# bf16 class value products, earlier loads for both attentions, and idle products around the stage boundaries

## The reference, cut to what matters

```python
h = _L0_tok_ref(x, weight, weighted_sum)                 # (8, 512, 256)
h = concatenate([broadcast(cls_tok), h], axis=1)         # (8, 513, 256)
h = h + _L0_attn_ref(_layernorm(h), ...)    # layernorm, masked product, 16 heads of 16, relu attention, MLP
h = h + _L0_ffn_ref(_layernorm(h), ...)     # fp4-quantized gated MLP, 704 wide
h = h + _L1_attn_ref(_layernorm(h), ...)    # conv, scan over the sequence, gate
h = h + _L1_ffn_ref(_layernorm(h), ...)     # softmax attention + top-2 of 8 experts

# causal attention of layer 0
att = relu(q @ k.T / 4) * tril(ones); att = att / (sum(att) + 1e-9); ctx = att @ v
# attention of the last layer
attn = softmax(q @ k.T / 4); attn_out = attn @ v
```

## Time and profile before

| | |
|---|---|
| median of 3 runs | 2316.9 us (2316.5 to 2319.5) |
| the profiled execution | 2317.53 us, span of the trace 2315.7 us |
| mean granted PE clock | 0.955 of full speed |
| PE / DVE / ACT / POOL busy | 92% / 69% / 39% / 29% |
| qkv | about 172 to 312 us |
| causal | 315 to 556 us |
| mlp, fp4 | 557 to 870, 871 to 1194 us |
| ssm_in and scan | 1195 to 1383 us |
| moe | 1384 to 1800 us |
| attend | 1801 to 2316 us |

### The profile page before, as it was taken

The page is one execution under the profiler, slowest core; times in us unless marked ns, Lnnn a source line. Parts: engine busy times, 40 slices in busy tenths (PEclk is TensorE's granted clock), DMA queues, the critical chain, the costliest instruction groups (busy, mean ns, idle before and its releaser), DMA issues. The chain is left out here.

```text
span 2315.7 us, 40942 instructions
## 1 busy us (share of the span) xinstructions
PE 2132.0 (92%) x11635; PEld 1349.1 (58%) x11635; DVE 1591.6 (69%) x4349; ACT 898.2 (39%) x2108; POOL 677.5 (29%) x1282
## 2 busy tenths in 40 slices
PE   7998969998999997999978949999999899999998
PEld 6877833334888885666653327888888223333332
DVE  3336846664777766888858856777776778888881
ACT  1114635553122224444424422222222067777777
POOL 3554525553333422333321101111111311111111
PEclk9998979998999999999989969999999589999999
DMA  3324664552000000000010001112212512222210
GB/s 126 117 86 94 150 183 131 139 138 89 1 0 0 0 0 14 0 0 0 0 54 9 9 27 38 43 40 46 46 38 45 141 34 75 75 75 75 75 43 20
DMA packets 215001, 131.95 MB, mean 57 GB/s; under 512 B 117186, under 2 KB 203916, under 8 KB 214924
## 3 DMA queue, kind: packets, MB, share of 16 engines
q1 hardware_dynamic: 214924, 131.01, 21.1%
HBM read 89.51 MB, written 40.93 MB: 56 GB/s over the span
## 5 line engine op out<-in xcount | busy, mean ns | idle before, releaser
L2474 DVE TENSOR_REDUCE attend_mx<-ps 128x1 f32<-128x512 f32 x512 | 326.0, 683 | 71.7 <-PE ps L2195 70.3
L2332 ACT ACTIVATE keep_x<-ps 128x512 f32<-128x512 f32 x512 | 280.7, 596 | 125.4 <-PE ps L2209 123.9
L1839 PE MATMUL ps<-keep_early,moe_zT 128*128 128x256 f32 x1056 | 243.3, 384 | 6.4 <-DVE keep_h L1994 4.4
L1839 PEld LDWEIGHTS ps<-keep_early,moe_zT 128*128 128x128 f32 x1056 | 196.5, 191 | 43.1 <-DVE keep_h L1994 18.6
L2195 PE MATMUL ps<-attend_ks,keep_o 96*128 96x512 bf16 x512 | 209.4, 414 | 9.0 <-DVE attend_mx L2474 4.7
L2209 PE MATMUL ps<-keep_o,attend_ks 99*128 99x512 bf16 x512 | 191.9, 384 | 2.2 <-ACT keep_x L2332 2.2
L857 DVE SCALAR_TENSOR_TENSOR keep_early<-ps,causal_causal 128x512 f32<-128x512 f32 (+3 forms) x256 | 114.1, 486 | 82.9 <-PE ps L737 82.8
L1994 DVE SCALAR_TENSOR_TENSOR keep_h<-ps,moe_g,keep_h 128x256 f32 (+1 forms) x264 | 127.5, 483 | 61.1 <-PE ps L1839 52.7
L2195 PEld LDWEIGHTS ps<-attend_ks,keep_o 96*128 96x128 bf16 x512 | 50.4, 99 | 195.9 <-DVE attend_mx L2474 148.9
L827 POOL TENSOR_TENSOR keep_early<-keep_early,causal_causal 128x128 f32<-128x128 f32 x256 | 113.0, 457 | 131.8 <-ACT keep_early L796 130.8
L796 ACT ACTIVATE keep_early<-ps 128x512 f32<-128x512 f32 (+3 forms) x256 | 98.5, 435 | 129.1 <-PE ps L737 128.9
(11 more groups left out here) (325 smaller groups left out, 4024.8 us busy)
## 6 DMA issues: line engine op xcount, KB each, us to landing
tok_xin<-in_xk SPq DMA_DIRECT2D x64, 256.0 KB, 2.8
qk_parts<-qkv_parts SPq DMA_DIRECT2D x33, 384.0 KB, 3.2
qk_parts<-moe_parts SPq DMA_DIRECT2D x33, 384.0 KB, 3.2
causal_qs<-qk_parts SPq DMA_DIRECT2D x96, 128.0 KB, 2.6
causal_ks<-qk_parts SPq DMA_DIRECT2D x96, 128.0 KB, 2.7
keep_o<-qk_parts SPq DMA_DIRECT2D x96, 128.0 KB, 2.8
attend_ks<-qk_parts SPq DMA_DIRECT2D x96, 128.0 KB, 2.8
v_all<-qkv_v SPq DMA_DIRECT2D x33, 136.0 KB, 3.1
```

The lines of the kernel that those rows point to most:

```text
L1839: last = nc.tensor.matmul(ps[:, E0 + pair % 2, e % 2 * D:(e % 2 + 1) * D], zT[:, u, k * P:(k + 1) * P], we[e][:, k, :], start=(k == 0), st ...
L2332: nc.scalar.activation(w[:, j, kt % 2, :], ps[:, SC + (HG * k + j) % RING, :], ACT.Exp)\
L2474: nc.vector.tensor_reduce(mx[:, t, k:k + 1], ps[:, MX + (TB * k + t) % RING, :], AX, ALU.max)\
```

## The change

1. *The class value product in bf16, in causal and attend.* The class weights and the class values are split into three bf16 parts, six pairs are stacked (48 rows in causal, 72 with gaps in attend), so L742 and L2216 become bf16 products. In qkv ACT writes the weights twice (fp32 and bf16) and POOL forms the two other parts; `cls_w` in DRAM gives way to `cls_parts`. The block diagonal matrices are made in DRAM (`diag_parts`, `diag`), which the first stage blanks, and are loaded. A half's load in causal now has six class loads of 8 rows where there was one of 16; `LOADS` goes from 14 to 19. In attend the pick products and the DVE multiplications go away, DVE's `largest` has three subtractions for one, POOL has four more operations a unit (`class_weights`), ACT one more Exp.
2. *Loads early.* Half 0 of image 0, the causal mask and the constants of the class product are loaded within qkv's last six tiles, the four head buffers of attend within moe's last six tiles (`LATE`), into memory reserved for that.
3. *Idle products.* `env.busy(bank, n)` issues n fp32 products of 128 x 128 x 128, whose results nobody reads: 12 at the end of tokens, qkv, causal, mlp, fp4, ssm_in, scan, moe and 12 at the start of qkv (16 more before its folded weights are ready), causal, mlp, fp4, ssm_in, scan and moe, 196 in all. None stand inside a stage's loops, none at the start of attend.

```diff
@@ pass_qkv, SP
+                sp.dma_start(io["cls_parts"][:, :, s - 1, :].rearrange("c h t -> h c t"), cls_p[:, u, :, :])\
+                    .then_inc(s_cout[u], 16)
-            for s, u, n in tiles(sp, 5):
+            for s, u, n in tiles(sp, 5, LATE):
...
-                if known(s) >= 1:
-                    class_out(s, u)
+                if known(s) >= 2:
+                    class_out(s - 1, 1 - u)
...
+                if isinstance(s, int) and s == NT - LATE:
+                    for w in range(2):
+                        sp.wait_ge(s_out[w], 16 * 3)
...
+                    ahead.first.load_stacks(sp, io, 0)
+                if isinstance(s, int) and s == NT - LATE + 1:
+                    sp.wait_ge(s_diag, 16 * 6)
+                    ahead.first.load_values(sp, io, 0)
+                    ahead.load_constants(sp, io)
@@ pass_qkv, PE
+            env.busy(0, 12)
             pe.wait_ge(s_rep, 1)
...
+            env.busy(0, 16)
             pe.wait_ge(s_fold, 1)
@@ class Half
+    def load_values(self, sp, io, b):
+        heads = slice(self.n * HALF, (self.n + 1) * HALF)
+        sp.dma_start(self.v[:, :, :], io["v_all"][bass.ds(1 + TB * b, TB), :, heads.start * (HD + 1):heads.stop * (HD + 1)]
+                     .rearrange("n p f -> p n f")).then_inc(self.sem, 16)
+        for c, part in enumerate(PQ):
+            sp.dma_start(self.cls[HALF * c:HALF * (c + 1), :],
+                         io["cls_parts"][part, heads, bass.ds(TB * b, TB), :].rearrange("h n t -> h (n t)"))\
+                .then_inc(self.sem, 16)
+LOADS = 3 * len(PQ) + 1
@@ pass_causal
+            halves[1].load_stacks(sp, io, 0)
+            halves[1].load_values(sp, io, 0)
...
                     sp.wait_ge(s_pv, STEPS * (b - 1) + STEPS // 2 * (half + 1))
-                    load_half(sp, io, b, half, qs[:, half], ks[:, half], v[:, half], cls_w[:, half, :], s_load[half])
+                    halves[half].load_stacks(sp, io, b)
+                    halves[half].load_values(sp, io, b)
...
-                nc.tensor.matmul(ps[:, 4 + g % 2, :], vbd[:, HG * g:HG * (g + 1), :].rearrange("h a d -> h (a d)"),
-                                 cls_w[:, g // 2, :], start=True, stop=False, skip_group_check=True)
+                nc.tensor.matmul(ps[:, 4 + g % 2, :], vb[:, g // 2, at:at + 2 * HD * HG], halves[g // 2].cls[:, :],
+                                 start=True, stop=False, skip_group_check=True)
@@ pass_moe, SP
+                unit = s - (NT - LATE) if isinstance(s, int) else -1
+                if unit == 0:
...
+                    env.heads.load_class(sp, io)
+                if 0 <= unit < 4:
+                    env.heads.load(sp, io, unit // 2, unit % 2, unit)
@@ pass_attend
-            pe.wait_ge(s_w, 48)
-            for b in range(B):
-                past(pe, s_vbd, b - 1)
-                nc.tensor.matmul(ps[0:HALF, MX + b % 2, 0:2 * VW], pick[:, b, :], v0[:, :], start=True, stop=True)\
-                    .then_inc(s_vb, 1)
...
+                    nc.tensor.matmul(ps[:, CTX, :], vb[:, b, half, 2 * HD * HG * g:2 * HD * HG * (g + 1)],
+                                     cwp[:, half, :], start=True, stop=False, skip_group_check=True)
...
+                    nc.scalar.activation(cw[:, :], turned[0:CR, :], ACT.Exp)
+                    nc.scalar.activation(cwp[:, u, :], turned[0:CR, :], ACT.Exp).then_inc(s_cw, 1)
@@ emit
+        def busy(bank, n):
+            for _ in range(n):
+                nc.tensor.matmul(env.ps[:, bank, S - P:S], env.ident[:, :], env.ones[:, :], start=True, stop=True)
```

More of the change, by code:

```diff
@@ new lines, with __init__, reserve, load_constants @@
+LOADS = 3 * len(PQ) + 1
+class Causal:
+    def __init__(self, nc):
+        self.area = Area(nc, "first")
+        self.s_load, self.s_const = self.area.sems("load", 2), self.area.sem("const")
+    def reserve(self):
+        self.first = Half(self.area, 0, self.s_load[0])
+        self.causal = self.area.sb("causal", [P, S])
+        self.vb = self.area.sb("vb", [HALF * len(PQ), 2, HALF * 2 * HD], BF16)
+    def load_constants(self, sp, io):
+        sp.dma_start(self.causal[:, :], io["causal"]).then_inc(self.s_const, 16)
+        for c, part in enumerate(PK):
+            sp.dma_start(self.vb[HALF * c:HALF * (c + 1), :, :],
+                         io["diag_parts"][part, 0, :, 0:HALF * HALF * 2 * HD].rearrange("a (h x) -> h a x", h=HALF))\
+                .then_inc(self.s_const, 16)
@@ L703, in _ @@
         def _(sp):
-            sp.dma_start(v0[:, :], io["v_all"][0]).then_inc(s_w, 16)
-            sp.dma_start(own[:, :, :], io["own"].rearrange("h (g d) -> h g d", d=HD + 1)).then_inc(s_w, 16)
-            sp.dma_start(pick[:, :], io["row_pick"][:, 0:NH]).then_inc(s_w, 16)
-            sp.dma_start(causal[:, :], io["causal"]).then_inc(s_w, 16)
-            for half in range(2):
-                load_half(sp, io, 0, half, qs[:, half], ks[:, half], v[:, half], cls_w[:, half, :], s_load[half])
+            halves[1].load_stacks(sp, io, 0)
+            halves[1].load_values(sp, io, 0)
+            sp.dma_start(v0[:, :], io["v_all"][0, 0:B, :]).then_inc(s_w, 16)
             env.ahead["mlp"].start(sp)
@@ L1027, in _ @@
         def _(pe):
+            env.busy(X2, 12)
             pre.wait(pe)
@@ L1501, in _ @@
         def _(pe):
+            env.busy(5, 12)
             pre.wait(pe)
@@ L2030, with __init__, load, load_class @@
 MAXIMA = 4 * HALF
+VW = HALF * (HD + 1)
+LOADED = 16 * (2 * len(PQ) + 1)
+class Heads:
+    def __init__(self, env, keep):
+        rows = HD * len(PQ) + 3
+        self.qs = env.o.bitcast(BF16)[0:rows, 0:NT - 1, :].rearrange("p (a h) t -> p a h t", a=4)
+        self.ks = env.x.bitcast(BF16)[0:rows, 0:NT - 1, :].rearrange("p (a h) t -> p a h t", a=4)
+        early, at = env.early[1], 0
+        self.v = early[:, at:at + 4 * TB * VW].rearrange("p (a t f) -> p a t f", a=4, t=TB)
+        at += 4 * TB * VW
+        self.room = early[:, at:at + 3 * S].rearrange("p (a t) -> p a t", t=S)
+        at += 3 * S
+        self.v0 = early[0:B, at:at + 2 * VW]
+        at += 2 * VW
+        self.own = early[0:HALF, at:at + VW].rearrange("h (g d) -> h g d", d=HD + 1)
+        self.s_load, self.s_w = keep.sems("load", 4), keep.sem("heads_w")
+    def load(self, sp, io, b, half, buf):
+        for c in range(len(PQ)):
+            for m, dst, part in ((half, self.qs, PQ[c]), (2 + half, self.ks, PK[c])):
+                src = io["qk_parts"][part, m, :, bass.ds(1 + TB * b, TB), :].rearrange("(h d) n t -> d h (n t)", d=HD)
+                sp.dma_start(dst[c:HD * len(PQ):len(PQ), buf, :, :], src).then_inc(self.s_load[buf], 16)
+        sp.dma_start(self.v[:, buf, :, :], io["v_all"][bass.ds(1 + TB * b, TB), :, half * VW:(half + 1) * VW]
+                     .rearrange("n p f -> p n f")).then_inc(self.s_load[buf], 16)
+    def load_class(self, sp, io):
+        sp.dma_start(self.v0, io["v_all"][0, 0:B, :]).then_inc(self.s_w, 16)
+        sp.dma_start(self.own, io["own"][0:HALF, 0:VW].rearrange("h (g d) -> h g d", d=HD + 1)).then_inc(self.s_w, 16)
 class Slot:
@@ L2157, in _ @@
                     sp.sem_inc(s_took, 1)
-                    load(x.b(-2), x.half(2), x.buf(2))
+                    heads.load(sp, io, x.b(-2), x.half(2), x.buf(2))
                 if x.has(1):
@@ L2537, in build @@
         w.lower = w.row(io["lower"])
+        env.heads = Heads(env, keep)
+        env.s_blank = keep.sem("blank")
         for step in PASSES:
-            step(nc, env, io)
+            if step is pass_qkv:
+                env.causal = Causal(nc)
+                with env.causal.area.ctx:
+                    env.causal.reserve()
+                    pass_qkv(nc, env, io)
+                    pass_causal(nc, env, io)
+            elif step is not pass_causal:
+                step(nc, env, io)
 PASSES = [pass_constants, pass_tokens, pass_qkv, pass_causal, pass_mlp, pass_fp4, pass_ssm_in, pass_scan, pass_moe,
```

306 lines of the change are left out of this document (203 added, 103 removed).

## The result

The changed kernel took 2360.96 us (median of 4 runs, 2359.77 to 2365.14) beside 2318.2 for the one before: a ratio of 1.0188, 95% interval 1.017 to 1.0206. It is slower, as forecast, but by 43 us where 10.7 were forecast, and outside the stated range of 2303 to 2345.

The account below looks back on a forecast made before the run. PE was taken as the bound in attend, SP's queue of loads in causal (13.8 us a half). Terms -26 - 9.5 + 38 - 3 - 1 + 9.7 + 2.5 = +10.7 on 2317.5 gave 2328 us, range 2303 to 2345.

Parts of the forecast that it names:

- Small: Start and qkv tiles: blanking the scratch +1.5 us, extra ACT and POOL operations +1, lying beside busy PE.
- 8.5 in the tail: End of qkv: half 0's 26 early load issues among the last tiles' stores delay causal's start by 8.5 us.
- Loads of a half, +38: Causal: five more class loads lengthen SP's queue, +2.7 us a half over 14 halves, +38 (ends +15 and +52).
- rival 1: Causal: the five loads are mostly hidden, 1.1 us a half, +15 instead of +38, total 2305; chance 0.25.
- Rival 2: Neither stage pays for loads; causal gains its 26 - 1 us too, total 2265; chance 0.05.
- Rival 3: Causal: PE's clock falls in every half's gap, 3.8 us more, +53 instead of +38, total 2343; chance 0.14.
- the net -3: Half 0's loads moved into qkv's tail: later causal start against a faster first half, -3 us (-10 to +5).
- the -9.5: Attend's loads moved into moe's tail: -11.6 us at attend's start, +1.9 for idle products ending moe (-12 to -4).
- Idle products, +9.7: Stage borders: the 196 idle products cost more than the clock they give back, sum +9.7 us (+3 to +20).
- Rival 4: Stage borders: idle products don't hold the clock and only cost, +8 us, total 2336; chance 0.08.
- Halves 16 to 17 us apart: Causal, profile after: PE's halves start 16 to 17 us apart; 14 us would mean the load term is wrong.
- A bracket of 4 to 5 us at a half's first score: Causal, profile after: PE waits 4 to 5 us for the class load at each half's first score.

Follow-up runs that it names:

- run 2: Changed kernel with one POOL operation replacing three on qkv's class weights: one tile later 2314.5 us, ratio 0.9978; in the old place 2331.05 us, 1.0053.
- run 8: Changed kernel with class parts one tile later and half 0, mask and class constants loaded at causal's start again: 2328.5 us, ratio 1.0043.
- run 5: Kernel before, with five more 8-row loads into an unread buffer in every causal half, class product still fp32: 2338.71 us, ratio 1.0091.
- run 7: Changed kernel, class parts one tile later, six class loads merged into three, causal's values and class loads issued by ACT from image 1: 2296.6 us, ratio 0.9907.
- run 4: Changed kernel's attend and early loads in moe only; qkv and causal as in the kernel before, no idle products: 2282.72 us, ratio 0.9843.
- run 3: Changed kernel with class parts one tile later and all 196 idle products left out: 2313.34 us, ratio 0.9981.
- run 11: Changed kernel without idle products, class parts one tile later, class loads merged into three, causal's values and class loads on ACT: 2286.4 us, ratio 0.9853.

## Why the prediction was wrong

**The sign came right by luck, and one term was far too small.** Without what qkv's tiles lost, the sum would have come out the other way: with the place mended and one operation for three (run 2), all the rest of the change takes 0.9978 of the time before. The step that failed is the last of the parts, *Small*: "the extra ACT and POOL operations of qkv's tiles +1 (in a steady stretch PE is busy 60.00 of 60.00, ACT 37.63, POOL 35.69, so they lie beside it)". It compared busy shares and did not ask what the new instruction waits for, nor what is queued behind it on POOL. What stood there: the next tile's root, and through it the whole tile. Measured: +63.8 us in qkv against +9.5 forecast for it (8.5 in the tail, 1 in the tiles). Of these the place and the three operations are worth 51.1 together (changed kernel less the late one-operation run), 34 to 37 for whichever is mended first and 14 to 17 for the other; the early loads are worth 7.8 (run 8, against 8.5 forecast for the tail); 5 are left, which no run takes apart.

**Loads of a half, +38: the mechanism was right, the size was not.** Measured +1.2 a half and not +2.7, by itself in run 5 and by the rows in the changed kernel. The issue of the five came to 1.87 instead of 2.4, the small ones landed 1.18 sooner instead of 0.2, the clock cost 0.9 in every second half on the mean (0.4 to 0.5 a half; 0.5 was taken). So it came out at the bound of rival 1 (1.1 a half), but not for the reason given there, since the issues were hidden by nothing. Rival 2 is excluded by run 5. Rival 3, the clock falling in every gap, happened in part, at the first scores of five of the seven halves from the `first` buffers read above, and was worth about 6 us (7 x 0.9), not 15. The prediction also says there that the trace of before bears such a fall only at stage borders; its own row of 1402 lies 18 us inside moe.

The sentence of the Trainium skill's "DMA: Bandwidth & Descriptors" ("Issuing engines are not separate DMA queues"), that initiating is usually small beside the transfer, would have put this term near zero. Runs 5 and 7 go against it here: five more issues, 1.9 us of SP's queue, cost 1.2 a half, and moving four issues to a second engine gave 33 us in the stage. Its other half, that the transfers themselves share the same engines, changed nothing visible at a DMA share of 0.59 in run 7's causal window.

**The rest of causal** was forecast, for the stage by itself, at about +27 (the loop's +38, less 11.5 at the start, since 8.5 of the net -3 lay in qkv's tail, less 1 at the end, and 1.2 for the border); it came out at +6.1: 14 x 1.2 = +17 for the loop, about -11 for the first half, whose loads had landed before the stage began (run 8: 11.4).

**Attend was right.** The stage itself was forecast at -26 - 11.6 = -37.6 (the +1.9 in the -9.5 lies in moe) and came out at -36.3: a start 11.8 us earlier against 11.6, and a unit at 27.17 against my 26.9, so 16 units gave 22.6 and not 26. It needs no idle products (run 4).

**Idle products, +9.7, were nearly right as a sum**: run 3 gives 13.4 and run 11 against run 7 gives 12.5. The borders of mlp, fp4 and ssm_in were put at +8.2 together and cost 6.8 in these three stages (run 3: 2.1, 4.5, 0.2) beside a share of causal's 3.4. Rival 4, that they give nothing back, put them at +17.7; the stages in which they show a net gain are qkv with 2.4 us and attend with 1.0, and what they give back inside the other stages' costs no run shows.

**What the stated signs said.** Halves 16 to 17 us apart: no, 15.0. A bracket of 4 to 5 us at a half's first score: no, 2.56 and 0.43 in the rows above. Class loads named in it: yes. SP's nineteen issues in 11 to 12 us: yes, 509.08 to 520.69. Attend's unit 26.9: nearly, 27.17. No sign had been stated for qkv's tiles, and so nothing on record would have caught that term.

## What to carry to other kernels

Before an operation is added to an engine that has time to spare, write down what it waits for and what stands behind it in that engine's queue; if the two are links of one chain, the loop closes and its whole length becomes the period, whatever the busy shares say. The sign of it in a profile is that all engines become less busy at once. One more turn of distance opens the loop at no cost in work (here 37 of 51 us); after that the queue of the engine that got the operations can still be the longest, its waits for its own results counted in. And a saving on the engine that looks busiest is worth nothing while a queue of loads paces it: look at the bracket of its first instruction in a period, and shorten the queue by a second issuing engine first.

## What the runs showed of the hardware

- Loads of 8 rows of 1 KB were issued 0.39 us apart, one of 16 rows of 2 KB held the queue for 0.44, the values (272 KB) for 0.46. Merged loads that repeat their source rows held it for 0.82 (24 rows), 0.69 (16) and 0.32 (8), so that three of them (2.23) saved nothing on six (2.31).
- Where the last load of a half had 8 rows (8 KB), PE went on 1.28 us behind the end of its issue; where it had 16 rows (32 KB), 2.46.
- Two dependent POOL operations on the same rows are 0.17 to 0.18 us apart, and 0.32 or more pass before the next one where the code waits for the last of them.
- ACT's issues of 0.42 and 0.76 us lie beside its activations: the relu behind the first one waited 0.18 us for it (run 7).
